# A fused attention and routed FFN kernel: gamma and beta on the turned rows, W1 split by GpSimd, W2 and vectors fetched per tile

## The reference, cut to what matters

```
x = x + _layernorm(_L0_attn_ref(_layernorm(x), w_kv_down, w_kv_up, w_q, w_out))   # 16 heads of 64, causal
x = x + _layernorm(_L0_ffn_ref(_layernorm(x), centroids, gamma, beta, W1, b1, W2, b2))

def _sublayer(xs, g, b, W1e, b1e, W2e, b2e):      # one expert
    mu = jnp.mean(xs, axis=-1, keepdims=True)
    var = jnp.mean(jnp.square(xs - mu), axis=-1, keepdims=True)
    h = (xs - mu) * jax.lax.rsqrt(var + EPS) * g + b
    return xs + jax.nn.relu(h @ W1e.T + b1e) @ W2e.T + b2e
expert = argmax(feats @ centroids.T)              # one expert for each token
alpha  = sigmoid(sum(feats * centroids[expert]))
out    = alpha * y[expert] + (1 - alpha) * feats
```

## Time and profile before

| what | value |
|---|---|
| median of 3 runs | 1282.72 us (1281.11 to 1283.78) |
| profiled execution | 1293.47 us, its span 1291.7 us |
| mean granted TensorE clock over the span | 0.975 |
| busy, PE / DVE / ACT / POOL | 96% / 88% / 85% / 72% |
| attention iteration in the loop | 16 slots |
| FFN tiles | 39 |

### The profile page before, as it was taken

The page is one execution under the profiler, slowest core; times in us unless marked ns, Lnnn a source line. Parts: engine busy times, 40 slices in busy tenths (PEclk is TensorE's granted clock), DMA queues, the critical chain, the costliest instruction groups (busy, mean ns, idle before and its releaser), DMA issues.

```text
span 1291.7 us, 41267 instructions
## 1 busy us (share of the span) xinstructions
PE 1234.7 (96%) x12456; PEld 1102.4 (85%) x12456; DVE 1136.6 (88%) x4481; ACT 1093.5 (85%) x3283; POOL 925.5 (72%) x1495
## 2 busy tenths in 40 slices
PE   7989999999999999999999999999999998889982
PEld 6878888888888888888898888988888888768871
DVE  5999999999999999999999999999999894588873
ACT  5989999999999999999999999999999882778871
POOL 4567777777777777777777777777777663367766
PEclk8999999999999999999999999999999996899996
DMA  5000000000000000000000000000000002523320
GB/s 227 6 10 18 17 16 16 16 16 16 16 16 16 16 16 16 16 16 16 16 16 15 16 14 15 15 16 16 16 16 13 15 15 71 161 84 101 97 81 17
DMA packets 39240, 43.09 MB, mean 33 GB/s; under 512 B 4802, under 2 KB 35398, under 8 KB 38800
## 3 DMA queue, kind: packets, MB, share of 16 engines
q1 hardware_dynamic: 33536, 29.43, 7.4%
q0 software_dynamic: 5648, 13.00, 2.7%
HBM read 25.16 MB, written 18.16 MB: 34 GB/s over the span
## 4 chain that ended last, share of the span: by engine, by line
PE 84%; issue 5%; DVE 4%; POOL 3%; ACT 2%; DMA 0%; another core or an unknown queue 0%; ACTq 0%; POOLq 0%; DVEq 0%
PE psZU L774 17%; PE psS L697 14%; PE psZU L789 14%; PE psP L741 9%; PE psZU L777 7%; PE psT L711 5%; PE psT L712 4%; PE psT L713 4%; PE psT L330 2%; PE psS L310 2%; POOL out L538 2%; PE psP L676 1%; PE psM L820 1%; PE psM L811 1%; PE psT L687 1%
## 5 line engine op out<-in xcount | busy, mean ns | idle before, releaser
L1293 POOL TENSOR_TENSOR softmax<-softmax,rinv 128x256 f32<-128x256 f32 (+1 forms) x512 | 413.8, 830 | 220.4 <-DVE rinv L1027 219.6
L865 ACT ACTIVATE softmax<-softmax,nmax 128x128 f32<-128x128 f32 (+1 forms) x1024 | 454.3, 452 | 17.0 <-DVE nmax L1003 16.7
L1003 DVE CUSTOM_DVE_ANT_0 softmax<-psS,mask 128x128 f32<-128x128 f32 (+1 forms) x1024 | 321.6, 352 | 9.2 <-PE psS L697 1.9
L1012 DVE TENSOR_TENSOR p_both<-psP,p_both 128x768 fp32r<-128x768 f32 x256 | 243.7, 952 | 3.6 <-ACT p_both L829 3.6
L829 ACT ACTIVATE t_hi<-psT 128x512 fp32r<-128x512 f32 x256 | 153.0, 598 | 82.7 <-PE psT L713 79.0
L829 ACT ACTIVATE p_both<-psP 128x768 fp32r<-128x768 f32 x256 | 206.5, 807 | 7.7 <-PE psP L741 7.7
L991 DVE TENSOR_TENSOR t_lo<-psT,t_hi 128x512 fp32r<-128x512 f32 x256 | 175.6, 686 | 37.4 <-ACT t_hi L829 37.3
L865 ACT ACTIVATION_READ_ACCUMULATOR softmax<-softmax,nmax 128x1 f32 x1024 | 200.4, 196 | 0.0
L1032 DVE TENSOR_TENSOR z_lo<-psZU,z_hi 128x512 fp32r<-128x512 f32 x256 | 175.3, 685 | 26.1 <-ACT z_hi L829 24.3
L697 PE MATMUL psS<-t_hi,t_lo 64*128 64x128 f32 (+1 forms) x1024 | 165.4, 318 | 1.7 <-DVE nmax L1003 1.7
L774 PE MATMUL psZU<-p_both,xk_hi 128*128 128x512 f32 x512 | 162.1, 398 | 0.0
(11 more groups left out here) (212 smaller groups left out, 3215.2 us busy)
## 6 DMA issues: line engine op xcount, KB each, us to landing
softmax<-routed_rows SPq DMA_DIRECT2D x39, 260.0 KB, 2.7
routed_rows<-padr SPq DMA_DIRECT2D x8, 520.0 KB, 5.0
wx<-ffn_w SPq DMA_DIRECT2D x2, 2058.0 KB, 12.9
xin<-x SPq DMA_DIRECT2D x32, 128.0 KB, 2.1
xres<-x SPq DMA_DIRECT2D x32, 128.0 KB, 2.0
out<-wq_s,ids POOLq DMA_INDIRECT x78
wup_s<-wup SPq DMA_DIRECT2D x1, 1024.0 KB, 5.0
routed_rows<-pay,dst POOLq DMA_INDIRECT x64
```

What stands on the lines that cost most here:

```text
L865: last = nc.scalar.activation(prob[:, pb, h, a:z], nscore[:, (s - lag) % 2, h, a:z], ACT.Exp, bias=nmax[:, pb, h, q:q + 1], scale=-1.0, ac ...
L1003: last = v.tensor_tensor_reduce(nscore[:, n1, h, a:z], psS[:, h, a:z], mask[:, a:z], -1.0, -MASKED, ALU.add, ALU.min, nmax[:, p1, h, q:q + 1])
L1012: v.tensor_tensor(by_half(p_lo, s % 2), psPh, by_half(p_hi, s % 2).bitcast(F32), ALU.subtract).then_inc(S["p_split"], 1)
L1293: last = g.tensor_tensor(pr, pr, rinv[:, p2, :, q:q + 1].broadcast_to([P, 2, z - a]), ALU.mult)
```

## The change

What it does:

1. **Gamma and beta on the turned rows.** ACT's `nt_hi` is now gamma times the turned rows plus beta. A new ACT instruction, `off` = beta - `nt_hi` (128 x 256), stands behind `yt`; DVE's `nt_lo` is gamma times the turned rows plus `off`, and it waits for `off_ready`. `first_bias`, the addition to b1 and the scaling of W1 are gone.
2. **W1 split by GpSimd.** In slot 9 of each of the 16 iterations GpSimd casts a 128 x 256 piece of W1 and subtracts (one piece is a sixteenth of all).
3. **W2 and vectors by transfer.** SP fetches gamma, beta, b1, W2 and b2 of a tile's expert from `wr` into `wst`, both in SBUF, 128 x 519 numbers a tile (266 KB), on the semaphore that also counts the tile's rows. The first eight such transfers are issued ahead of the first eight row loads; each later one follows its row load. ACT's copy `w2st` is gone.
4. **First table.** It is made from the counts three blocks old, in 17 small parts in slots 7 to 15 of the last iteration and the drain slots 0 to 5; the table is ready in drain slot 2. A wait between two steps stands ahead of the second step and no longer behind the first. The late table has six parts, behind FFN slots 9 to 14.
5. **Last alpha.** The exponential of the last block is a power on GpSimd, no longer ACT's Exp.
6. **Smaller.** DVE's `carry` copy is a wait by itself; all 45 FFN slots are written out, on each engine.

```diff
@@ FFN on SP
+            def weights(m0, s):
+                e = sp.value_load(table[0:1, bass.ds(m0 + s, 1), 1], min_val=0, max_val=E - 1)
+                sp.dma_start(wst[:, s], wr[:, bass.ds(e, 1)].rearrange("p a c -> p (a c)")).then_inc(f_loaded[s], 16)
+
+            for s in range(FU):
+                weights(0, s)
+            sp.wait_ge(S["pt_ready"], 2 * PAIRS * NB)
+            sp.wait_ge(S["rows_written"], 16 + 32 * (NB - 3))
...
-                if s == 0 and not live(1):
-
-                    sp.wait_ge(S["pt_ready"], 2 * PAIRS * NB)
-                    sp.wait_ge(S["rows_written"], 16 + 32 * (NB - 2))
                 sp.dma_start(fin[:, s], rows[bass.ds(row, T), :].rearrange("(t p) c -> p t c", p=P)
                              ).then_inc(f_loaded[s], 16)
+                if live(FU):
+                    weights(m0, s)
@@ FFN on PE
-            pe.wait_ge(S["bias_added"], 1)
...
-                    pe.wait_ge(f_loaded[s], n0 + 16)
+                    pe.wait_ge(f_loaded[s], 2 * n0 + 32)
@@ FFN on ACT
-                    cp(nt_hi[:, s % 2, :], psN[:, 0:T]).then_inc(S["nt_hi_done"], 1)
+                    nc.scalar.activation(nt_hi[:, s % 2, :], psN[:, 0:T], ACT.Identity, scale=wst[:, s, 0:1],
+                                         bias=wst[:, s, BETA:BETA + 1]).then_inc(S["nt_hi_done"], 1)
...
+                if live(0):
+                    act.wait_ge(S["nt_hi_done"], m0 + s + 1)
+                    nc.scalar.activation(off[:], nt_hi[:, s % 2, :].bitcast(F32), ACT.Identity, scale=-1.0,
+                                         bias=wst[:, s, BETA:BETA + 1]).then_inc(S["off_ready"], 1)
...
-                    cp(w2st[:, s % 4, :], wx[:, bass.ds(e, 1), B1:].rearrange("p a c -> p (a c)")
-                       ).then_inc(S["w2st_ready"], 1)
@@ FFN on DVE
-                    dve.wait_ge(S["nt_hi_done"], m0 + s + 1)
+                    dve.wait_ge(S["off_ready"], m0 + s + 1)
                     if live(2):
                         dve.wait_ge(S["h_done"], m0 + s - 1)
-                    v.tensor_tensor(nt_lo[:, s % 2, :], psN[:, 0:T], nt_hi[:, s % 2, :].bitcast(F32),
-                                    ALU.subtract).then_inc(S["nt_ready"], 1)
+                    v.scalar_tensor_tensor(nt_lo[:, s % 2, :], psN[:, 0:T], wst[:, s, 0:1], off[:], ALU.mult,
+                                           ALU.add).then_inc(S["nt_ready"], 1)
@@ first iteration on ACT and DVE, drain slots on PE
-                    nc.scalar.activation(w1[:, e, 0, :], wx[:, e, 0:FB * P], ACT.Copy,
-                                         scale=gam[:, e:e + 1]).then_inc(S["w1_hi_done"], 1)
...
-                if not live(0) and 1 <= s <= E // 2:
-                    first_bias(range(2 * s - 2, 2 * s))
@@ attention slots on GpSimd
+                if s == PAIRS + 1 and live(0):
...
+                    g.tensor_copy(part, piece).then_inc(S["w1_hi_done"], 2)
+                    wait_apart(pool, S["w1_hi_done"], b0 + 2)
+                    g.tensor_tensor(low, piece, part.bitcast(F32), ALU.subtract).then_inc(S["w1_split"], 2)
```

More of the change, by code:

```diff
@@ L1 @@
+import math
 from contextlib import ExitStack
@@ L231, in ffn_phases @@
         def ffn_phases(eng, slot, behind):
-            rest = TILES % FU
-            for k in range(EARLY):
-                slot(k // FU * FU, k // FU * 16, k % FU, lambda lag: k >= lag)
+            for k in range(TILES + 6):
+                if k == EARLY:
+                    eng.wait_ge(S["table_ready"], 2)
+                slot(k // FU * FU, k // FU * 16, k % FU, lambda lag: lag <= k < TILES + lag)
                 behind(k)
[L238 to L248, removed]
         def pad(eng, experts):
@@ L389, in link, with running_sum @@
             ins.then_inc(S["table_steps"], 1)
-            nc.vector.wait_ge(S["table_steps"], tables[0])
-        def running_sum(buf, src):
-            for n, d in enumerate((1, 2, 4)):
-                nc.vector.tensor_copy(buf[:, n, 0:d], src[:, 0:d])
-                link(nc.vector.tensor_tensor(buf[:, n, d:E], src[:, d:E], src[:, 0:E - d], ALU.add))
-                src = buf[:, n, :]
+        def running_sum(buf, n, src):
+            v, d = nc.vector, 1 << n
+            v.tensor_copy(buf[:, n, 0:d], src[:, 0:d])
+            link(v.tensor_tensor(buf[:, n, d:E], src[:, d:E], src[:, 0:E - d], ALU.add))
         def early_table(part):
@@ L491, in slot @@
                     last.then_inc(S["g_steps"], 1)
-                    dve.wait_ge(S["g_steps"], 2 * m + 2)
-                    v.tensor_copy(carry[:], gst[:, 0, 0:1])
+                    wait_apart(dve, S["g_steps"], 2 * m + 2)
                     for t in range(2):
@@ L681, in _ @@
             pe.wait_ge(S["qk_split"], 3)
-            def first_bias(experts):
-                for e in experts:
-                    for j in range(FB):
-                        last = mm(psT[:, 0, e * FB + j:e * FB + j + 1], wx[:, e, j * P:(j + 1) * P], bet[:, e:e + 1],
-                                  start=True, stop=True)
-                last.then_inc(S["bias_done"], 1)
             def scores(tb):
@@ L909, in slot @@
                     exps(0, 1)
-                if r == 5 and live_b(2):
+                if r == 5 and live_b(2) and not (db == 1 and not live(0)):
                     act.wait_ge(S["argmax_steps"], 3 * (b0 + db) - 5)
@@ L1090, in misc_early @@
                 r, db = s % PAIRS, s // PAIRS
-                if not live(0) and s == 5:
-                    dve.wait_ge(S["bias_done"], E // 2)
-                    b1v = wx[:, :, B1:W2]
-                    v.tensor_tensor(b1v, psT[:, 0, 0:E * FB].rearrange("p (e j) -> p e j", e=E), b1v,
-                                    ALU.add).then_inc(S["bias_added"], 1)
                 if r == 2 and live_b(2):
@@ L1262, in slot @@
                     g.tensor_tensor(idf[:, db, :], idf[:, db, :], two_t[:], ALU.add)
+                if r == 5 and db == 1 and not live(0):
+                    pool.wait_ge(S["argmax_steps"], 3 * NB - 2)
+                    g.tensor_tensor(ea[:], inv_e[:], best[:], ALU.pow).then_inc(S["exp_done"], 1)
                 if r == 5 and live_b(-1):
```

139 lines of the change are left out of this document (88 added, 51 removed).

## The result

The changed kernel is slower: 1308.43 us as a median (1305.67 to 1308.71, 4 runs) against 1282.36 for before on the same chip, a ratio of 1.0177 with a 95% interval of 1.014 to 1.0214. A second series (experiment e11) gave 1307.27 against 1284.35, and the same ratio, 1.0177 (1.0146 to 1.0207). The direction was forecast, the size was too small: +13.7 forecast, 23 to 26 measured. 1308.43 lies 0.4 us above the top of the prediction's eight-in-ten range (1308), and 5 above the range of its own forecast (1289 to 1303).

The account below looks back on a forecast made before the run. PE was taken to bind the attention and FFN loops, with no slack for a later `nt_lo`. -6.5 - 7.8 - 0.4 + 28.4 + 0 = +13.7 on the median 1282.72 gave 1296.4 us, eight in ten 1279 to 1308.

Parts of the forecast that it names:

- A: First attention iteration: without DVE's scaling of W1, eight early slots fall from 39.11 to 32.61 us; -6.5 us.
- B: First FFN tile: `first_bias` goes, but the first row load queues behind eight weight fetches on SP; -7.8 us.
- C: FFN slots 0 to 3, at low clock and filled with drain work: one wait fewer; -0.4 us.
- D: FFN slots, tile 4 to 38: `nt_lo` 0.98 us later passes to PE, slots 3.96 to 4.94; +28.4 us.
- E: Emptying from tile 38 on: GpSimd's scatters bind as before; 0 us, bounds -3 to +1.
- The slot has no reserve against a later `nt_lo`: FFN slot: a late `nt_lo` lengthens the slot one for one, read from slots 11 (0.59 us) and 13 (0.85).
- Nothing in these stages is gained: Attention loop and FFN loop: PE busy 110.00 of 110.00 and 39.26 of 40.00 us, so relieving ACT, DVE or GpSimd gains nothing.
- a measurement of this kernel tells 0.2%: Whole kernel: a measurement can tell 2.6 us from no change, which is 1280.2 to 1285.3 us.
- R1: FFN slots: the late `nt_lo` wait is hidden and slots stay at 3.96; 1263 us, middle form 1280; chance 0.13.
- R2: SP's weight fetches are cheap, the first tile gains 14.8 us and no fetch stalls; 1287 us; chance 0.12.
- R3: FFN: longer waits drop PE's clock to 0.50 for ten slots, +24 us; 1320 us; chance 0.06.
- R4: FFN: the 266 KB SBUF-to-SBUF fetch binds all slots at 5.5 us or more; 1313 us; chance 0.04.

Follow-up runs that it names:

- e11: The changed kernel timed again with no edit, beside before's runs on the same chip: 1307.27 us, ratio to before 1.0177.
- e3: Changed kernel with ACT's `off` moved ahead of `yt`: 1301.02 us, ratio to before 1.0068.
- e5: Changed kernel with a second, unused ACT instruction like `off` ahead of it: 1320.28 us, ratio to before 1.0266.
- e7: Kernel before with DVE's gating moved ahead of the low part `nt_lo`: 1273.24 us, ratio to before 0.9914.
- e8: Changed kernel with DVE's gating ahead of the low part, and weights and rows issued tile by tile for the first eight tiles: 1264.84 us, ratio to before 0.983.
- e9: Kernel before without the 64 `first_bias` matmuls and the addition to b1: 1278.52 us, ratio to before 0.995.
- e6: Changed kernel with SP issuing weights and rows tile by tile for the first eight tiles, not eight weight fetches first: 1297.63 us.
- e4: Changed kernel with DVE's gating of tile k-4 moved ahead of the low part of tile k: 1280.45 us, ratio to before 0.9914.
- e1: Kernel before, unchanged, profiled a second time (the second profile): 1285.03 us.
- e2: Changed kernel with turned rows copied and subtracted as before, without gamma, beta and `off`: 1277.50 us, ratio to before 0.9896.

## Why the prediction was right in direction and short in size

- *The sum.* By terms, forecast and then measured against the first profile and the second: A -6.5, -5.9, -6.2; B -7.8, -4.7, +4.8; C -0.4, -0.2, +0.5; D +28.4, +25.5, +24.0; E 0, +0.2, +0.2. That the first sum, 14.9, comes so near 13.7 is partly luck: B was forecast 3.1 us too favourably and D 2.9 too dearly, and the two nearly cancel.
- *Bound of the FFN.* "The slot has no reserve against a later `nt_lo`" was right, and the two slots read from the trace gave the slope of one that e3 and e5 confirm. "Nothing in these stages is gained" as long as PE is busy was wrong for the FFN: PE was 8% under its pace at 98% busy, held by the very gate that the prediction followed (turn-back at +1.92, where e7 has +1.64), and e7 took that without taking work from any engine.
- *A, scaling of W1.* The mechanism was right: the eight slots of the earlier trace rows take 31.79 now, 7.3 less, and 3.92 to 4.08 each. In this execution they began 2.8 later than before (52.93 against 50.18), with the granted clock at 0.66 from 30 to 40 us, and the last turn of the attention comes 5.9 to 6.2 earlier. In e8, with the same attention and a clock of 1.00 from 10 to 50 us, it comes at 1038.0, 8.7 earlier. GpSimd's split cost nothing that can be seen: 200 us windows between 190 and 900 us hold 2177 to 2182 matmuls in both kernels. The eight slots and the next eight, changed kernel:

```profile
52.93:84.72 31.79, 31.79 (x344) 28.52 (x343) 29.80 (x110) 29.48 (x91) 19.31 (x29) 1.00 0.01 2
84.72:117.31 32.59, 32.59 (x357) 29.20 (x356) 30.86 (x123) 29.41 (x94) 25.31 (x41) 1.00 0.06 18
```

- *B, first tile.* This step failed in its size. It was forecast at -7.8. Behind the end of the attention the changed kernel needs 42.9 us to the first tile: 4.7 less than the first profile of before, but 4.8 more than the second. Its mechanism (rows ninth on SP's queue) was right, and the weight fetches took 1.2 us each as assumed. Two things were not. "Now the table is ready one slot or more earlier; I take 1073" starts SP's queue 26.3 us behind the last `fn` turn; it started 29.6 behind (1070.39 against 1040.8), 3.3 later, which accounts for the 3.1 that B lacks against the first profile (the fetches took 0.8 more than counted, and the first rows 3.0 from issue to turn where 1.2 + 2.7 was counted). And what the fetches were compared with was a drain at half clock from 1073 on, which makes the other 9.5. e9 shows that the removal of `first_bias` is worth 3 us where the clock falls late, and e6 that the order of the fetches costs 9.
- *C, slots 0 to 3.* 18.3 us, against 18.5 and 17.8: as forecast, about nothing.
- *D, slots.* Sized well: 4.90 for 4.94, and +24.0 to +25.5 for +28.4. What the new kernel has beyond 34 equal slots is 169.1 - 34 x 4.90 = 2.5, not 4.1; 1.3 of it is the slot of tile 16, the first of the late table (6.17). The `remote` wait of 2.6 and 3.3 us (see e4) is in both profiles of before and not in this one; without it D might have come nearer the forecast.
- *E, emptying.* 0.2, as good as the 0 forecast.
- *From the profile to the median.* This is the step that made the forecast short. The difference between two executions was carried over to the median of before as if the long fall of the clock were part of both. Before's profiled execution had it (1293.47); the four timed executions beside the result, 1281.11 to 1283.78, show nothing of that size. The mismatch of 10.75 us stood in the text and was treated as an offset. Read as a warning it gives, after the fact, 13.7 + 10.75 = 24.5, if none of before's long fall is in the changed kernel; measured 23 to 26. The answer depends on the series, though: beside the 1292.82 of e1 to e4 a changed kernel of 1307 to 1308 would cost only 14 to 16 us, an estimate, since it was not timed there. For the same reason "a measurement of this kernel tells 0.2%" was wrong: before's median moved by 10 us from series to series.
- *Rivals.* R1 is out by the slots of 4.90 and by e2 and e5. R2 is out: the fetches held up the first tile for 7.80 us. R3 is out, PEclk is 1.00 from tile 4 to tile 38. R4 is out: PE's only wait for a transfer in the FFN is that of the first tile.

Why DVE's instruction of the earlier trace rows took 742 ns once and 1596 at the median was not tested by a run of its own; the counts of matmuls in the loop leave no room for a cost there in part A.

The pointer operands, cited from the Trainium skill (ScalarE: Activation LUTs, "What ACT_TABLE_LOAD costs"), came out: `nt_hi` with two of them lasts 0.57 in this trace (0.566 at the median of 39), against the prediction's estimate of 0.58 from the page, and 0.39 in before's copy without.

## What to carry to other kernels

Where an engine's in-order stream puts an instruction that gates PE behind one that has a slot of slack, price the gate's chain and not the engine's load, and try the other order first: here one swap on DVE was worth 27 us in the changed kernel and 12 in the old. An engine at 98% busy in a profile may still be held by such a gate; count its instructions in a window, and try whether another order raises the count, before calling it the bound. If the profiled execution is not near the median of the runs, find out what it has that they lack before any term is taken from it.

## What the runs showed of the hardware that had not been expected

- The granted clock of the transition varied between executions of one kernel: in the same window, 0.76 in one and 0.99 in the next, with the same busy time and 184 against 232 matmuls. The stretch up to the first tile differed by 9.5 us between the two profiles, the kernel by 8.4, and all timed executions by 14; how much of the 14 is the clock's is not shown. In the first profile the lower level (1.2 of 2.4 GHz) began at 1073, and PE had been busy for 23.85 of 25 us around it in both executions; why it began there in one and about 12 us later in the other was not settled. From 1074 to 1095 in the first profile PE was busy for all 21.00 us, at a granted clock of 0.50 throughout.
- An ACT instruction that reads the result of the one ahead of it, and waits for its semaphore, started 0.14 us later than an independent one (0.60 in e3 against 0.46).
- A queue of eight fetches from SBUF to SBUF, 266 KB each, took SP 9.5 us, 1.2 each, about as long as row loads from DRAM (8.46 for eight), and landed 2.8 us behind their issue, the row loads 2.9. At 4.90 us a slot the two transfers a tile cost nothing that shows; in e8's slots of 3.6 four turns waited for `wst`, 3.4 us in sum.
